# First attention: two of eight heads of the ring's query blocks written by GpSimd instead of ScalarE

## What is computed

```python
v = (values @ Wv + bv).reshape(N, K, H, D)      # N 8, Q = K = 128, H 16, D 8
k = (keys @ Wk + bk).reshape(N, K, H, D)
q = (queries @ Wq + bq).reshape(N, Q, H, D)
rel = rel_emb[idx].reshape(Q, K, H, D)
energy = jnp.einsum('nqhd,nkhd->nhqk', q, k)
energy = energy + jnp.einsum('nqhd,qkhd->nhqk', q, rel)
energy = jnp.where(mask == 0, jnp.float32(-1e+20), energy)
attn = jax.nn.softmax(energy / jnp.sqrt(jnp.float32(D)), axis=3)
out = jnp.einsum('nhqk,nkhd->nqhd', attn, v).reshape(N, Q, E)
out = out * after_mask
return out @ Wo + bo
```

## Time and profile before

| what | value |
|---|---|
| median of three runs | 407.36 us (407.35 to 408.51) |
| profiled execution | 407.63 us, of which its span (first to last instruction) 405.6 us |
| busy PE, PEld | 353.1 us (87%), 252.6 us (62%) |
| busy DVE | 333.5 us (82%) |
| busy ACT | 301.1 us (74%) |
| busy POOL | 61.1 us (15%), 48 instructions |
| line 1409 on ACT | 23.2 us of busy time in its larger group, mean 980 ns |
| mean granted TensorE clock | 0.979 of full speed |

### The profile page before, as it was taken

The page is one execution under the profiler, slowest core; times in us unless marked ns, Lnnn a source line. Parts: engine busy times, 40 slices in busy tenths (PEclk is TensorE's granted clock), DMA queues, the critical chain, the costliest instruction groups (busy, mean ns, idle before and its releaser), DMA issues.

```text
span 405.6 us, 10259 instructions
## 1 busy us (share of the span) xinstructions
PE 353.1 (87%) x4047; PEld 252.6 (62%) x4051; DVE 333.5 (82%) x716; ACT 301.1 (74%) x732; POOL 61.1 (15%) x48
## 2 busy tenths in 40 slices
PE   2899999998967688998698889899999999998676
PEld 1498888887742334555455556576667767676565
DVE  4989987896477989979689999989898999995433
ACT  1689999896375427776757878898989898986563
POOL 2000002000203021000033033204032323221110
PEclk9999999999989989999999999999999999999869
DMA  8800010000000000000000000000000000000000
GB/s 309 354 4 3 4 42 3 3 4 3 2 0 2 0 1 2 0 2 2 0 2 2 1 2 1 2 0 2 1 2 2 1 2 2 1 2 0 2 27 26
DMA packets 1774, 8.29 MB, mean 20 GB/s; under 512 B 192, under 2 KB 448, under 8 KB 1472
## 3 DMA queue, kind: packets, MB, share of 16 engines
q1 hardware_dynamic: 1728, 7.65, 4.8%
HBM read 7.12 MB, written 0.52 MB: 19 GB/s over the span
## 4 chain that ended last, share of the span: by engine, by line
PE 43%; DVE 27%; ACT 18%; issue 10%; DMA 1%; DVEq 0%; ACTq 0%
PE ps L250 16%; ACT PT L1529 5%; ACT blk L1409 3%; DVE PT L1225 3%; DVE lneg L1209 3%; PE ps L511 3%; PE ps L625 3%; DVE blk L1183 2%; PE ps L661 2%; DVE ss_floor L1193 2%; ACT PT L1599 2%; PE ps L377 2%; PE ps L498 2%; PE ps L587 2%; PE ps L615 2%
## 5 line engine op out<-in xcount | busy, mean ns | idle before, releaser
L1733 POOL TENSOR_TENSOR blk<-blk 128x1024 f32<-128x1024 f32 x16 | 37.8, 2360 | 169.1 <-DVE blk L1187 169.1
L1529 ACT ACTIVATE PT<-ps,lneg 128x128 f32<-128x128 f32 x128 | 45.2, 379 | 5.3 <-DVE lneg L1209 5.3
L573 PE MATMUL ps<-w_f,full 128*128 128x512 f32 x96 | 47.3, 609 | 0.9 <-issue 0.9
L250 PEld LDWEIGHTS ps<-blk,st 128*128 128x128 bf16 x768 | 26.8, 98 | 3.8
L1043 DVE TENSOR_REDUCE mneg<-ps 128x4 bf16<-128x512 bf16 x32 | 22.0, 688 | 8.2 <-PE ps L355 7.9
L1529 ACT ACTIVATION_READ_ACCUMULATOR PT<-ps,lneg 128x1 f32 x128 | 28.0, 219 | 0.0
L250 PE MATMUL ps<-blk,rel 128*128 128x64 bf16 x768 | 27.6, 193 | 0.0
L250 PE MATMUL ps<-blk,st 128*128 128x64 bf16 x768 | 27.6, 193 | 0.0
L1586 ACT ACTIVATE PT<-ps 128x512 f32<-128x512 f32 x32 | 17.4, 594 | 12.9 <-PE ps L511 12.9
L1209 DVE TENSOR_REDUCE lneg<-ps 128x8 f32<-128x1024 f32 x16 | 19.6, 1223 | 8.6 <-PE ps L250 8.5
L1225 DVE TENSOR_TENSOR PT<-PT,lrec 128x512 f32<-128x512 f32 x32 | 25.3, 790 | 1.1
(11 more groups left out here) (234 smaller groups left out, 911.7 us busy)
## 6 DMA issues: line engine op xcount, KB each, us to landing
w_f<-f_dram SPq DMA_DIRECT2D x2, 1689.0 KB, 13.4
w_x<-l_dram SPq DMA_DIRECT2D x1, 774.0 KB, 6.1
w_f<-ffn_dram SPq DMA_DIRECT2D x1, 561.0 KB, 8.1
X<-x_dram SPq DMA_DIRECT2D x1, 512.0 KB, 3.7
ctxT<-ctxT_dram SPq DMA_DIRECT2D x1, 512.0 KB, 4.6
OT<-maskT_dram SPq DMA_DIRECT2D x1, 512.0 KB, 7.2
rest<-l_dram SPq DMA_DIRECT2D x1, 385.0 KB, 4.8
const<-const_dram SPq DMA_DIRECT2D x1, 324.0 KB, 6.4
```

The costliest lines, as they stand in the source:

```text
L250: return mm(out, l, r, start=start, stop=False, skip_group_check=True)
L573: m = mm(ps[:, c, :], hT[:, n, :], w_f[:, l, F_QKV + 512 * c:F_QKV + 512 * (c + 1)], start=True, stop=True)
L1529: e = a(S1[:, i % 2, P * k:P * (k + 1)], ps[:, 3 + c, P * j:P * (j + 1)], ACT.Exp, bias=lneg[:, i % 2, k:k + 1], accum_out=lsum[:, i % 2, ...
L1733: g_.tensor_tensor(R[:, i % 2, :], R[:, i % 2, :], T2, ALU.add).then_inc(sem("pair_sum"), 1)
```

## The change

`set_ring_ends` moves from ScalarE's list to GpSimd's. ScalarE's loop loses its two copies per block and the two waits ahead of the first. GpSimd now waits for `query_high` and for the first ring write, and then writes heads 6 and 7 of blocks 3 to 31 in a loop of its own, each as a product with the mask's column and with 1.0. Because it doesn't run in step with the scores, it has a wait of its own before blocks 4 to 31: that the block four before, whose slot it takes, is scored. Its bias sum, which waited for 18 scored blocks, now follows the loop in its list, with no wait on `scores` of its own. VectorE's and TensorE's code is the same.

```diff
--- before.py
+++ after.py
@@ -1400,19 +1400,6 @@
                 act.wait_ge(sem("o_ps"), 2 * g + c + 1)
                 a(OA[:, c, :], ps[:, 6 + c, :], ACT.Copy).then_inc(sem("oa_taken"), 1)
 
-            def set_ring_ends(c):
-                g, q = c // NCH, (c % NCH) * QC
-                if c == NCH:
-                    act.wait_ge(sem("query_split"), 1)
-                src = (part, part1)[g][:, :, :].rearrange("p b (n t) -> p (b n) t", n=NB)[:, :, q:q + QC]
-                for h in range(HD, HG):
-                    i = a(ring[:, c % RING, :, :, :, h].rearrange("p b n q -> p (b n) q"), src, ACT.Copy,
-                          scale=const[:, C_ROWMASK + h:C_ROWMASK + h + 1])
-                i.then_inc(sem("ring_ends"), 1)
-
-            act.wait_ge(sem("query_high"), 1)
-            act.wait_ge(sem("ring"), 1)
-            set_ring_ends(RING - 1)
             for i in range(G * NCH + 2):
                 if i == 8:
                     act.wait_ge(sem("ffn0_in"), 16)
@@ -1422,8 +1409,6 @@
                     if i >= 2:
                         act.wait_ge(sem("turned"), i - 1)
                     a(St_b[:, i % 2, :], ps[:, i % 4, :], ACT.Copy).then_inc(sem("st_copied"), 1)
-                if i >= 1 and i + RING - 1 < G * NCH:
-                    set_ring_ends(i + RING - 1)
                 if i >= 2:
                     c, q = i - 2, (i - 2) % NCH * QC
                     act.wait_ge(sem("shifted"), c + 1)
@@ -1696,8 +1681,23 @@
                 pool.wait_ge(sem("y"), y)
                 g_.tensor_tensor(X[:, :, :], X[:, :, :], row(bo), ALU.add).then_inc(sem("bias_added"), 1)
 
+            def set_ring_ends(c):
+                g, q = c // NCH, (c % NCH) * QC
+                if c >= RING:
+                    pool.wait_ge(sem("scores"), c - RING + 1)
+                if c == NCH:
+                    pool.wait_ge(sem("query_split"), 1)
+                src = (part, part1)[g][:, :, :].rearrange("p b (n t) -> p (b n) t", n=NB)[:, :, q:q + QC]
+                for h in range(HD, HG):
+                    i = g_.tensor_scalar(ring[:, c % RING, :, :, :, h].rearrange("p b n q -> p (b n) q"), src,
+                                         const[:, C_ROWMASK + h:C_ROWMASK + h + 1], 1.0, ALU.mult, ALU.mult)
+                i.then_inc(sem("ring_ends"), 1)
+
             pool.wait_ge(sem("l0_in"), 16)
-            pool.wait_ge(sem("scores"), NCH + 2)
+            pool.wait_ge(sem("query_high"), 1)
+            pool.wait_ge(sem("ring"), 1)
+            for c in range(RING - 1, G * NCH):
+                set_ring_ends(c)
             add_bias(0, w_x[:, A_BO:A_BO + P], NB)
 
             pool.wait_ge(sem("expd"), G * NCH)
```

## The result

The changed kernel takes 409.3 us (median of 17 runs) against 407.36 us (also of 17), 1.9 us more. One of its runs lasted 682 us and is left out of the ratio, which is taken over the other runs and isn't that of the two medians: 1.0066, 95% interval 1.0047 to 1.0085. By it the kernel is slower by about 2.7 us (1.9 to 3.5). The profiled execution took 409.11 us, its span 407.3 us.

A forecast was written before the change was run, and what follows sets the result against it. The prediction took ScalarE, then nearly full VectorE, to bound the score loop. Block 14's delay +4.3, blocks 15 to 19 -0.8 and the moved sum +1.6 made +5.1 us: 412.5 us against 407.36, range 406.4 to 417.5.

The forecast's parts named there:

- The bound: First attention's score loop: ScalarE holds blocks back by about 0.2 us each, but VectorE, nearly as full, decides block 14's start.
- The exposure per pair, 15 x 0.40 us: Blocks 3 to 17's pairs each stop VectorE 0.40 us: 6.0 us, less 1.7 slack, so block 14 starts 4.3 us late.
- The bound "nothing": Lower limit of the exposure per pair: every GpSimd pair lies beside a VectorE reduction; the upper limit was the full 0.88 us.
- The price of a pair, 0.88 us: GpSimd's two ring products per block take 0.44 us each, between 0.68 and 2.2 us a pair, well inside 2.06 a block.
- Blocks 15 to 18 and 19, -0.8 us: Block steps there shrink to 2.06 us, gaining 0.7 us, and 0.1 more as the sum no longer stalls block 19's ring write.
- Blocks 19 to 26 at nothing: TensorE sets the pace there; pairs meeting the weights' quantisation add up to 3.2 us, as much as is free, taken as 0.
- The moved sum, +1.6 us: Near 89.4 us the 2.37 us bias sum holds up dense VectorE work; less a 0.69 us reduction, 1.6 us reaches the loop's end.
- The sum of parts: Whole kernel: +4.3 - 0.8 + 1.6 = +5.1 us on the profiled execution, 412.5 us predicted for the median.
- Out of phase everywhere: Rival: pairs always fall between a block's scores and the ring write, nothing is exposed; faster, 405.7 us; chance 0.12.
- A wash: Rival: exposure of 0.2 us per pair, +0.5 us, 407.9 us, and 1.6 more with the bias sum; chance 0.12.
- GpSimd as the bound: Rival: a pair takes 2.2 us, above 2.06 a block, so VectorE's writes wait for GpSimd; +14, 421.5 us; chance 0.08.

The follow-up runs named there:

- sum_end: The changed kernel with GpSimd's bias sum put behind the loop's last exponential; ratio 1.0034 (1.0006 to 1.0063) to the kernel before.
- the probe: The kernel before with the bias sum behind the loop and added GpSimd products and memsets into unused memory; executed once, only durations read, no time or ratio.
- sum_late: The kernel before, ScalarE keeping its ring copies, with only GpSimd's bias sum moved to wait for 28 scored blocks instead of 18; ratio 1.0056 (1.0024 to 1.0089).

## Why the prediction came out as it did

The direction and the range were right (slower, 409.3 within 406.4 to 417.5); the size was not, 5.1 us against 2.7 by the ratio, and the working behind it was wrong in its largest term. That the sum still came out on the right side is in part luck.

**The bound.** Right: VectorE decides block 14, and the gain from ScalarE's copies before it is small. Block 8, for one, starts 0.76 us earlier (38.08 against 38.84), and by block 12 that is gone.

**The exposure per pair, 15 x 0.40 us: the step that failed.** This term was to make block 14 start 4.3 us late; it came 0.42 us late. The timeline of VectorE, and one of GpSimd's products in the same stretch:

```profile
41.74 1.01 DVE L918 TENSOR_TENSOR blk<-part,const 128x768 bf16<-128x768 bf16 x1
42.68 0.41 DVE L909 COPY blk<-O 64x1024 bf16<-64x1024 bf16 x1
43.12 0.88 DVE L910 COPY blk<-O 64x1024 bf16<-64x1024 bf16 x1
...
44.75 0.96 DVE L918 TENSOR_TENSOR blk<-part,const 128x768 bf16<-128x768 bf16 x1
...
39.99 2.43 POOL L1692 TENSOR_SCALAR blk<-part,const 128x128 bf16<-128x128 bf16 x1 [0.15 <-PE ps L250]
```

The 13 ring writes of blocks 3 to 15 take 0.97 us on average instead of 0.95, 1.05 at most. One instruction, the copy at 43.12, takes 0.88 instead of 0.42. VectorE's ring write at 41.74 had started 0.29 us earlier than before, and block 14 starts 0.42 us later, so 0.71 us is lost between them: 0.46 in that copy, the rest in ring writes and a difference that last up to 0.1 us longer. That is about 0.05 us for each of the 15 pairs (an estimate), not 0.40. Nor did every one-operand instruction stand still: the copy at 42.68 and the casts at 37.94 and 48.23 keep their 0.41 and 0.68 to 0.69 us with a product of GpSimd beside them. It was GpSimd that paid: the product at 39.99 took 2.43 us. I read the earlier trace rows as "ring writes and GpSimd exclude each other", but that row has a sum with two operands of 1024 values. The small product hardly holds the ring write off. The bound "nothing" was in the text, and the row nearest in kind (a product with one operand and 128 values) was not in the trace; I took the value in the middle of two bounds where it lay at one end.

**The price of a pair, 0.88 us.** Somewhat low. Without anything beside it but a reduction and a ring write:

```profile
61.69 1.43 POOL L1692 TENSOR_SCALAR blk<-blk,const 128x128 bf16<-128x128 bf16 x2 [0.63 <-PE ps L250]
...
61.85 0.69 DVE L1043 TENSOR_REDUCE mneg<-ps 128x4 bf16<-128x512 bf16 x1 [0.50 <-PE ps L355]
62.46 0.95 DVE L918 TENSOR_TENSOR blk<-blk,const 128x768 bf16<-128x768 bf16 x1
```

The two records cover 1.43 us. Counted from start to start, as the work behind it sees it, the last pair takes 1.02 us (from 88.30 to the sum at 89.32), and products that follow each other without a wait start every 0.58 to 0.59 us (24.46, 25.05). It didn't matter for the time, for a pair has three blocks.

**Blocks 15 to 18 and 19, -0.8 us.** Right: they start 2.06 us apart, and from block 14 to block 19 it is 11.01 us instead of 11.70, 0.7 less.

**Blocks 19 to 26 at nothing.** Right.

**The moved sum, +1.6 us.** The mechanism and its place were right, and it is most of the loss; the size was off. The stall was 2.95 us, not 1.7, because the last ring pair stands ahead of the sum in the same list and VectorE's product found no gap between them; and TensorE's half clock came on top. From block 27 (0.27 us early) to block 31 (2.67 late) this part is 2.94 us. Not all of it is the sum's: in sum_end, which has the pairs but not the sum there, the same way is 0.95 us (0.17 early to 0.78 late). That is the last pair beside the quantising product, which the prediction had at nothing, and it leaves about 2 us for the sum with the half clock. The 0.65 us by which block 28 came earlier is swallowed, as the prediction had it.

**The sum of parts.** +0.42 - 0.69 + 2.94 = 2.7 us at the loop's end, against +4.3 - 0.8 + 1.6. Two errors of opposite sign partly cancelled: 3.9 us too much at block 14, 1.3 too little at the end. With the measured 0.42 in the first place the forecast's own sum would have been +1.2.

**The rivals.** "Out of phase everywhere" described the ring pairs' effect on VectorE up to block 27 well, for another reason than phase. It lost to the moved sum and to the last pair: without the sum (sum_end) the kernel was still about 1.3 us above before. "A wash" with the sum's price, 407.9 + 1.6 = 409.5 us, is the nearest of all to the measured 409.3, but through 3.0 us of exposure that wasn't there. GpSimd as the bound did not come true at two products, and did at four.

## What to carry to other kernels

When work goes to GpSimd, ask for each VectorE instruction beside it what form it has. In these runs a copy, cast or one-operand product could stand still through everything that GpSimd had queued (3.23 instead of 0.28 us), though several did not stand still at all; a two-operand one waited by more than 0.1 us only for instructions that read 1024 values. And look at what the moved work pushes along its new queue: here 2.4 us of bias sum, which nobody needed yet, landed beside dense work. Moving that sum and the dense quantisations turned a loss of 0.7% into a gain of 0.4%, while moving the quantisations in the kernel before gained nothing that its ratio can show (0.9993).

## What the runs showed that was not expected

- A small strided product of GpSimd (128 bf16 values) repeats every 0.58 us, more than half of one with 1024 contiguous f32 values (1.10 us), and beside VectorE's instructions in blocks 3 to 15 its record lasts 1.3 us on average and up to 2.69 us, against 0.84 to 0.99 from 54 us on.
- The stalls of the one-operand quantising product added up over queued GpSimd instructions (0.96 + 1.94 = 2.90 us, 2.95 measured); a two-operand ring write got in between two of them (1.27 us in the probe).
- A wait of 1.95 us of TensorE was followed by a stretch at half clock that cost the next block 1.3 us; in sum_late, waits of 0.61, 0.66 and 0.66 us within seven microseconds were not.
